# One DVE operation for the least scale and the difference, in the ternary weights of a macaron block

## The reference, cut to what matters

```python
def ternary_quant(w_fp32, g=64):
    w = w_fp32.astype(bfloat16)
    w_g = w.reshape(-1, g)
    scale = clip(mean(abs(w_g), axis=-1, keepdims=True), 1e-08, None)
    q = clip(round(w_g / scale), -1, 1)
    return (q * scale).reshape(w.shape)

def ffn(x, w_gate_up, w_proj):                 # 2048 tokens of 512, hidden size 2048
    gate, up = split(x @ ternary_quant(w_gate_up).T, 2)
    h = silu(gate) * up
    return rms_norm(h) @ ternary_quant(w_proj).T

x = x + 0.5 * ffn(layernorm(x)); x = x + attention(layernorm(x)); x = x + 0.5 * ffn(layernorm(x))
```

## Time and profile before

| what | value |
|---|---|
| time, median of 3 runs | 883.15 us (882.89 to 884.12) |
| the profiled execution's own time | 882.62 us |
| its span | 880.8 us |
| PE busy | 864.8 us, 98% of the span |
| DVE busy | 477.9 us, 54% |
| ACT busy | 399.2 us, 45% |

### The profile page before, as it was taken

How to read it: one execution, slowest core, us unless ns; L and a number is a source line. 1 busy time by engine, 2 the same in 40 slices (tenths; PEclk the granted TensorE clock), 3 DMA queues, 4 the chain that set the end, 5 groups by cost and what they waited for, 6 DMA issues and landing times.

```text
span 880.8 us, 12730 instructions
## 1 busy us (share of the span) xinstructions
PE 864.8 (98%) x4836; PEld 404.4 (46%) x4902; DVE 477.9 (54%) x911; ACT 399.2 (45%) x762; POOL 71.5 (8%) x106
## 2 busy tenths in 40 slices
PE   6999999999999999999999999999999999999998
PEld 5544444444444444444444444444444444444445
DVE  7999997824235455518393938544334444333232
ACT  6976667555344445232333325343344434433331
POOL 2211001100000000101000000000000100000000
PEclk9999999999999999999999999999999999999999
DMA  9999509995446677520202020063343334332336
GB/s 262 176 180 125 73 1 180 214 188 137 84 71 140 122 173 152 81 52 1 50 1 49 1 42 8 12 116 77 73 72 72 72 72 73 73 72 60 60 66 138
DMA packets 234829, 80.79 MB, mean 92 GB/s; under 512 B 221201, under 2 KB 224017, under 8 KB 234769
## 3 DMA queue, kind: packets, MB, share of 16 engines
q1 hardware_dynamic: 226944, 67.92, 40.8%
q0 software_dynamic: 3872, 4.72, 4.0%
q10 hardware_dynamic: 3952, 7.34, 2.5%
HBM read 25.43 MB, written 4.19 MB: 34 GB/s over the span
## 4 chain that ended last, share of the span: by engine, by line
PE 91%; DVE 4%; ACT 2%; DMA 1%; issue 1%; SPq 0%; DVEq 0%; ACTq 0%
PE proj_ps L1210 23%; PE up_ps L1196 22%; PE gate_ps L1196 21%; PE sum_ps L1333 5%; PE up_ps L1333 5%; PE gate_ps L1333 5%; PE proj_ps L1233 4%; PE proj_ps L1196 3%; PE sum_ps L1182 1%; PE gate_ps L1243 1%; DMA xs<-xn 1%; PE proj_ps L1346 1%; DVE stats L858 0%; DMA xs<-in_L_attn_x_dram 0%; DVE slots L1090 0%
## 5 line engine op out<-in xcount | busy, mean ns | idle before, releaser
L1210 PE MATMUL proj_ps<-down_w,slots 128*128 128x512 bf16 x909 | 202.7, 379 | 1.1 <-issue 0.2
L1196 PE MATMUL up_ps<-gu_w,xT 128*128 128x512 bf16 (+1 forms) x878 | 199.7, 367 | 1.8 <-DVE slots L884 0.8
L1196 PE MATMUL gate_ps<-gu_w,xT 128*128 128x512 bf16 (+1 forms) x878 | 199.8, 367 | 1.1
L884 DVE SCALAR_TENSOR_TENSOR slots<-up_ps,silu 128x512 f32<-128x512 f32 x117 | 80.8, 690 | 172.8 <-PE up_ps L1196 148.1
L631 ACT ACTIVATE silu<-gate_ps 128x512 f32<-128x512 f32 x117 | 69.0, 590 | 165.8 <-PE gate_ps L1196 165.6
L1210 PEld LDWEIGHTS proj_ps<-down_w,slots 128*128 128x128 f16 x928 | 90.7, 98 | 110.1 <-DVE xs L906 0.8
L1196 PEld LDWEIGHTS gate_ps<-gu_w,xT 128*128 128x128 f16 x896 | 85.5, 98 | 99.2 <-DVE gu_w L962 0.3
L1196 PEld LDWEIGHTS up_ps<-gu_w,xT 128*128 128x128 f16 x896 | 85.2, 98 | 99.2 <-DVE slots L884 1.3
L641 ACT ACTIVATE o_buf<-slots 128x512 f32<-128x512 f32 x128 | 80.4, 628 | 100.3 <-DVE slots L884 99.6
L897 DVE SCALAR_TENSOR_TENSOR slots<-slots,inv 128x512 f16<-128x512 f32 x124 | 91.1, 743 | 1.2 <-ACT slots L652 1.1
L652 ACT ACTIVATE slots<-slots,inv 128x512 f16<-128x512 f32 x124 | 86.5, 711 | 7.7 <-POOL inv L559 4.2
(11 more groups left out here) (138 smaller groups left out, 773.9 us busy)
## 6 DMA issues: line engine op xcount, KB each, us to landing
out_dram<-xs SPq DMA_DIRECT2D x15, 256.0 KB, 2.4
xs<-in_L_attn_x_dram SPq DMA_DIRECT2D x3, 1024.0 KB, 8.0
aw_raw<-in_L_attn_w_qkv_dram ACTq DMA_DIRECT2D x12, 256.0 KB, 2.8
slots<-in_L_ffn_w_gate_up_dram ACTq DMA_DIRECT2D x5, 512.0 KB, 6.6
aw_raw<-in_L_attn_w_qkv_dram SPq DMA_DIRECT2D x8, 256.0 KB, 3.0
aw_raw<-in_L_ffn_w_gate_up_dram POOLq DMA_DIRECT2D x4, 256.0 KB, 4.9
aw_raw<-in_L_ffn_w_proj_dram POOLq DMA_DIRECT2D x4, 256.0 KB, 5.6
aw_raw<-in_L_attn_w_proj_dram ACTq DMA_DIRECT2D x4, 256.0 KB, 2.6
```

The lines of the kernel that those rows point to most:

```text
L884: nc.vector.scalar_tensor_tensor(out=h_rows(i, q), in0=bank(up_ps, j), scalar=gu_out(i), in1=silu_rows(j), op0=ALU.mult, op1=ALU.mult).the ...
L1196: mm = nc.tensor.matmul(bank(ps, j)[:, first:first + width], xT(m)[:, t, r, k, :], gu_w[:, k, c:c + width], start=(k + r == 0), stop=(k == ...
L1210: mm = nc.tensor.matmul(proj_ps[:, use % 2, :], h_turned(i)[:, r, j, :], down_w[:, j, :], start=(r + j == 0), stop=(r == 1 and j == HC - 1))
```

## The change

The clip at the least scale and the subtraction become one instruction, `scalar_tensor_tensor`: (w_scale max LEAST) - w_size. The intermediate value is no longer written in bf16, so the constant is the bf16 value nearest to 1e-8. `least_scale` and its semaphore go; `difference` waits for `s_done` itself and stays where it was in the list.

```diff
+LEAST = 1.0011717677116394e-08
...
-            def least_scale(p):
-                if p < PIECES:
-                    dve.wait_ge(s_done, p + 1)
-                    nc.vector.tensor_scalar(w_scale[p % 3], w_scale[p % 3], 1e-8, None, ALU.max).then_inc(clip_done, 1)
-
             def difference(p):
-                dve.wait_ge(clip_done, p + 1)
-                nc.vector.tensor_tensor(w_scale[p % 3], w_scale[p % 3], w_size[p % 4], ALU.subtract)\
-                  .then_inc(diff_done, 1)
+
+                dve.wait_ge(s_done, p + 1)
+                nc.vector.scalar_tensor_tensor(out=w_scale[p % 3], in0=w_scale[p % 3], scalar=LEAST, in1=w_size[p % 4],
+                                               op0=ALU.max, op1=ALU.subtract).then_inc(diff_done, 1)
...
-            least_scale(0)
             difference(0)
...
                 sign_bits(p + 2)
-                if p != 7:
-                    least_scale(p + 1)
                 kept(p)
                 for q, i in made[1:2]:
                     hidden(i, q)
                 if p in FINAL_SOONER:
                     final_weights(p)
-                if p == 7:
-                    least_scale(p + 1)
                 if p + 1 < PIECES:
                     difference(p + 1)
```

More of the change, by code:

```diff
@@ L337, in macaron_kernel @@
         s_done = sem("s_done")
-        clip_done = sem("clip_done")
         diff_done = sem("diff_done")
```

## The result

The changed kernel takes 885.07 us (median of 17 runs, 884.64 to 885.79), the kernel before 883.04 us beside it. The ratio is 1.0023, with a 95% interval of 1.0016 to 1.0029: a loss of 2.0 us, small but clear of noise (1.4 to 2.6 us by the interval). The forecast was 884.0.

A forecast was written before the change was run, and what follows sets the result against it. Up to 51 us DVE's delay reaches PE nearly one for one: 4 x (0.20 + 0.13) = 1.3 us, 1.0 after small gains, 0.9 taken; span 880.8 to 881.7, median 884.0 us, range 882.3 to 885.8.

The forecast's parts named there:

- One column at a time: On DVE, the new operation takes 1.22 us, a step of 1.14, 0.20 us more than the two it replaces.
- the fast form: Rival: the new DVE operation runs at two columns, step 0.60, gaining 0.3 to 0.8 us: 882.6 us; chance 0.15.
- The lost cover: On DVE, pieces 0 to 3: without the clip between `near` and `kept`, the step is 0.73, not 0.60: 0.13 us more each.
- A part is absorbed: Up to PE's wait ending at 51.03 us: of DVE's 1.0 us delay a part can be absorbed, so 0.9 taken.
- Nothing behind 51 us: After 51 us PE loses nothing more: 1.10 us of DVE air per four pieces, of which the operations take 0.80.
- The bound of 1.21 us a step: Steady part behind 51 us: above this step DVE falls behind PE each round, which would turn the answer.
- Own time and median: Profiled execution: span from 880.8 to 881.7, own time from 882.62 to 883.5 us; median 0.5 above that, 884.0.
- a dearer operation: Rival: the new DVE operation has a step of 1.42, adding 1.7 us more up to 51 us: 885.8 us; chance 0.05.
- The highest chance, 0.74: Chance that the measured difference stays under 0.2%, 1.8 us; slower had 0.18, faster 0.08.
- The clock: Rival: PE's granted clock falls once more near 30 us, after a new gap at 28.5: 885.4 us; chance 0.12.
- the 0.2 us that the forecast set against the loss: DVE's wait for ACT ahead of one clip near the start, 0.2 us, counted against the added DVE time.
- The absorbed delay: Rival: up to 51 us, a later issue finds the full DMA engines freer and lands sooner: 883.2 us; chance 0.08.

The follow-up runs named there:

- one_op_last16: Kernel before with the one operation only for pieces 8 to 23, clip and difference kept for pieces 0 to 7: 882.93 us, ratio 1.0001.
- clip_too_last16: Kernel before, but pieces 8 to 23 keep the clip and also take the new operation for the difference: 884.04 us, ratio 1.0012.
- no_clip: Changed kernel with the least scale left out, only the difference of two tensors staying: 882.58 us, ratio 0.9999 to the kernel before.
- before_pad: Kernel before with a POOL memset put ahead of the load of piece 11, as a control: 883.57 us, ratio 1.0008.
- before_turn3_sooner: Kernel before with SP's transpose of the fourth token tile issued ahead of that of piece 10: 881.78 us, ratio 0.9989.

## Why the prediction held, and where its sum was off

- *One column at a time* (1.22 us, step 1.14): right, 1221 ns and 1.13. Choosing by the f32 rows of the same kind was enough; the fast form did not come. The Trainium skill leaves it possible in "VectorE: DVE Perf Modes", section "What auto-detection actually checks", if the firmware enables it. The trace shows 16-bit tensors and 1221 ns: this operation did not take columns in pairs.
- *The lost cover* (0.13 a piece): right in kind, mis-sized. The step from `near` to `kept` is 0.79 and not 0.73, so a piece pays 0.19. The 0.73 was read at another pair, `difference` and `over_half`; the same trace had 0.79 where `final_weights` follows `kept` bare, from the row below to 52.85. DVE's own delay came to 1.22 us, forecast 1.0: 4 x (0.20 + 0.19) = 1.56, less 0.28 for the step that had held the wait for ACT and 0.06 from the first piece.

```profile
52.06 0.68 DVE L948 TENSOR_TENSOR att_w<-att_w 128x1024 bf16<-128x1024 bf16 x1
```

- *A part is absorbed* (0.9 of 1.0): this step failed. DVE's wait for ACT ahead of the second `x_low` took in 0.20 (0.53 us before, 0.33 now), the price of piece 5's operation as reckoned, and nothing beyond, because ACT came as late as the rest: its silu of pair 0 started at 30.58 instead of 29.17. And instead of something being absorbed on the way through SP and the DMA engines, 0.86 us were added there: 0.71 in the issue of piece 10's transpose, 0.15 in the landing. The sum had every duration of SP's and the DMA engines' part unchanged. That is the larger part of the 1.1 us between forecast and measurement. Why they grew is open, as the controls above show.
- *Nothing behind 51 us*: right, by the stretches and by `one_op_last16`. The bound of 1.21 us a step, however, was no turning point. `clip_too_last16` has steps of 0.34 + 1.14 = 1.48, far over it, for a loss of 0.9 us. Whether DVE keeps up round by round matters less than how much it is behind when the pieces end.
- *Own time and median*: the profiled execution has a span of 883.1 us. The forecast of 881.7 missed the terms above and the 0.2 of the first input, 1.4 us in all. That the median missed by only 1.1 is chance: the forecast put it 0.5 above the profiled execution, and it lies 0.16 above (885.07 and 884.91).
- *Range and chances*: 885.07 lies in the range of 882.3 to 885.8, but 0.2 above the 884.9 that the forecast gave itself. The upper end was held open for a fallen clock and a dearer operation, and neither came; that the number fell inside is luck as far as that goes. The highest chance, 0.74, was for a difference under 1.8 us; it was 2.0, with an interval on both sides of that bound.
- *The rivals.* The fast form: its worth (0.3 to 0.8) is about what `no_clip` gives (0.5, not clear of noise), but it isn't what the chip does. The clock: it stayed at full speed (1.00) around PE's gap at 28.5 to 29.9, so this rival fell. From 15 to 17 us it was at 1.00 in the changed kernel's execution and at 0.50 in that of before. That is not the change's doing: it was at 1.00 in `before_pad` and `before_turn3_sooner` too. Nor does the likeness of two gaps, by which the forecast priced this rival, decide: in the changed kernel PE was busy for only 0.60 us of the 1.60 ahead of 15.00, and the clock did not fall. The low clock goes with the 0.2 us that the forecast set against the loss: DVE's wait for ACT in the row below is in the trace of before and not in those two. From DVE's first step on the weights to the final weights of piece 3 it is 14.39 us in the kernel before, 14.15 and 14.23 in those two and 15.61 in the changed kernel, so DVE's own delay is 1.22 against the one and 1.4 to 1.5 against the others. The absorbed delay: no.

```profile
19.54 0.43 DVE L929 TENSOR_SCALAR att_w<-att_w 128x1024 bf16<-128x1024 bf16 x1 [0.19 <-ACT att_w L694]
```

PE alone in the changed kernel, by stretch (us, busy, granted clock, DMA share, GB/s), the counterpart of the earlier trace rows:

```profile
15.00:17.00 2.00, 1.51 (x14) 1.00 1.05 121
...
27.00:29.00 2.00, 1.53 (x22) 1.00 0.89 195
```

What stays open is why the transposes behind piece 9 take some 0.8 us longer in the changed kernel; they also take longer in `before_pad`, where DVE is not late.

## What to carry to other kernels

Fewer instructions are not less time: an operation with a scalar and two tensors took 1.13 us a step here, where the two it replaced took 0.34 and 0.60 together, and it also took away the instruction that had covered the wait between its neighbours. Ask in which stretch the engine is on the chain: the same edit on 16 of 24 pieces cost nothing, on the first 8 it cost 1.8 us. And where the chain leads on through DMA engines that are full, don't carry their durations over unchanged: here the same stretch took 10.4 to 11.5 us from kernel to kernel, a spread of half of what the change cost. Look there for the order of issues first, since one number in SP's order gained 1.35 us by the medians.

## What the runs showed of the hardware that I had not expected

- A transpose of 128 x 1024 16-bit elements by DMA landed in anything from 3.0 to 8.1 us between 38 and 53 us of the span. Moving a load of 256 KB out of the way of one transpose (5.6 us to 3.0) let the next load start sooner, and another transpose took 8.1 us instead of 5.1.
- The step between two bf16 operations of which the second reads the first's result was 0.73 us at one place (53.91 to 54.64) and 0.79 at others (26.65 to 27.44, and 52.06 to 52.85 in the kernel before), where 0.60 is the step without that. What sets the one or the other is not known.
